# A two-layer graph transformer on one core: scores and values of two head pairs at a time

## What is computed

```
# layer 0: 8 heads of 64 features
Q, K, V = x @ W_q + b_q, x @ W_k + b_k, x @ W_v + b_v
scores = Q K^T / 8 + (a_i + c_j + b_g + log(adj + 1e-9))    # a, c = x @ w_g halves
x1 = softmax(scores) V + x
# layer 1: one head of 512 features, masked where adj == 0
scores = (x1 @ Wq + bq) (x1 @ Wk + bk)^T / sqrt(512)
ctx = softmax(masked scores) x1 @ Wc
out = layernorm(x1 + ctx) * gamma + beta
```

## Time and profile before

| | |
|---|---|
| median of three runs | 2368.58 us |
| time of the profiled execution itself | 2369.99 us |
| span of its profile, first to last instruction | 2368.2 us |
| PE busy | 2287.8 us (97%) |
| DVE busy | 1906.0 us (80%) |
| ACT, POOL busy | 1213.2 us (51%), 939.1 us (40%) |
| mean granted clock of PE | 0.989 of 2.4 GHz |
| DMA, mean share of its 16 engines | 35.9% |

### The profile page before, as it was taken

One profiled execution on the slowest core, in us unless ns is written; L12 is line 12 of the kernel. 1 busy time (PEld: TensorE's weight loads), 2 busy tenths in 40 slices (PEclk: granted clock), 3 DMA queues, 4 the chain that ended last, 5 costly groups with the idle time before them and its releaser, 6 DMA issues.

```text
span 2368.2 us, 39148 instructions
## 1 busy us (share of the span) xinstructions
PE 2287.8 (97%) x13268; PEld 1876.8 (79%) x13268; DVE 1906.0 (80%) x5507; ACT 1213.2 (51%) x3474; POOL 939.1 (40%) x1146
## 2 busy tenths in 40 slices
PE   7999999999999999999999999999999999999986
PEld 4788888888888888888888888888888888888874
DVE  4587888888888888888888888888888888887776
ACT  4545455545455545455545555544555554555542
POOL 0133345433345433445433444433444433344423
PEclk8999999999999999999999999999999999999997
DMA  6333343333343333343333334333334333333221
GB/s 223 107 94 118 123 125 120 121 107 111 121 134 121 115 113 109 124 134 121 107 121 107 125 123 131 100 123 113 125 124 130 99 120 117 124 122 127 88 81 45
DMA packets 187304, 277.97 MB, mean 117 GB/s; under 512 B 24672, under 2 KB 122592, under 8 KB 182880
## 3 DMA queue, kind: packets, MB, share of 16 engines
q1 hardware_dynamic: 187104, 275.47, 35.9%
HBM read 166.54 MB, written 108.86 MB: 116 GB/s over the span
## 4 chain that ended last, share of the span: by engine, by line
PE 72%; DVE 22%; POOL 3%; issue 1%; SPq 1%; DMA 0%; ACT 0%; DVEq 0%
PE bank L213 19%; PE bank L215 19%; PE bank L214 19%; PE bank L474 5%; PE bank L497 5%; PE bank L461 5%; DVE bias L942 4%; DVE x1n L1109 3%; DVE bnst L1112 3%; POOL probs L1247 3%; DVE xn L1004 2%; DVE probs L958 2%; DVE scratch L1001 2%; DVE turned L977 2%; DVE y_lo L1103 2%
## 5 line engine op out<-in xcount | busy, mean ns | idle before, releaser
L1247 POOL TENSOR_TENSOR probs<-probs,rcp 128x512 f32<-128x512 f32 x256 | 261.5, 1042 | 1184.5 <-DVE rcp L968 1184.5
L734 ACT ACTIVATE probs<-probs,nmax 128x128 f32<-128x128 f32 x1024 | 397.2, 391 | 264.0 <-DVE nmax L958 264.0
L1029 DVE STREAM_TRANSPOSE x1n<-x1T 32x512 f32<-32x512 f32 x512 | 359.8, 703 | 60.6 <-DMA out<-x1n 53.5
L755 ACT ACTIVATE g_sb<-bank,consts 128x512 f32<-128x512 f32 x128 | 88.1, 689 | 316.5 <-PE bank L215 314.7
L213 PE MATMUL bank<-wv_hi,x_hi 128*128 128x512 f32 x512 | 203.4, 397 | 34.1 <-DVE x1n L1109 32.6
L958 DVE CUSTOM_DVE_ANT_0 probs<-bank,bias 128x128 f32<-128x128 f32 x1024 | 227.2, 286 | 1.4
L1255 POOL TENSOR_TENSOR x_lo<-xT_land,x_hi 128x512 fp32r<-128x512 f32 x124 | 169.9, 1406 | 145.7 <-ACT x_hi L688 145.7
L213 PE MATMUL bank<-x_hi,wm_hi 128*128 128x512 f32 x512 | 205.6, 402 | 9.7 <-DVE x_lo L990 9.7
L977 DVE STREAM_TRANSPOSE turned<-probs 128x1024 f32<-128x1024 f32 x128 | 158.7, 1240 | 69.5 <-POOL probs L1247 68.5
L213 PE MATMUL bank<-x_hi,wk_hi 128*128 128x512 f32 x512 | 205.9, 402 | 7.3 <-DVE x_lo L901 7.3
L213 PE MATMUL bank<-wc_hi,x_hi 128*128 128x512 f32 x512 | 204.3, 399 | 0.0
(11 more groups left out here) (129 smaller groups left out, 5362.9 us busy)
## 6 DMA issues: line engine op xcount, KB each, us to landing
turn_dram<-turned SPq DMA_DIRECT2D x128, 512.0 KB, 2.6
probsT<-turn_dram SPq DMA_DIRECT2D x512, 128.0 KB, 2.7
out<-x1n SPq DMA_DIRECT2D x128, 256.0 KB, 2.2
xn<-in_x SPq DMA_DIRECT2D x126, 256.0 KB, 4.1
xT_land<-in_xT SPq DMA_DIRECT2D x31, 1024.0 KB, 5.2
adj_sb<-in_adj SPq DMA_DIRECT2D x32, 256.0 KB, 3.2
c_rows<-c_dram SPq DMA_DIRECT2D x32, 256.0 KB, 4.5
at_dram<-scratch SPq DMA_DIRECT2D x31, 256.0 KB, 2.0
```

Of the source, the lines that this page charges most:

```text
L734: op = nc.scalar.activation(probs[:, k, :], probs[:, k, :], ACT.Exp, bias=nmax[:, k:k + 1], scale=-1.0, accum_out=sums[:, k:k + 1])
L1029: op = nc.vector.transpose(x1n[b * BLK:(b + 1) * BLK, :, :] .rearrange("p g (c a s) -> p a c g s", c=C, a=P // BLK)[:, a, :, :, :], x1T[a ...
L1247: nc.gpsimd.tensor_tensor(probs[:, half, :], probs[:, half, :], rcp[:, half].unsqueeze(2).to_broadcast([P, HALF, P]), ALU.mult)\
```

## The change

PE does the scores and the values of two head pairs in one visit: `pv(u, 2)`, `pv(u, 3)`, `scores(t, 0)`, `scores(t, 1)` in the first, and `pv(t, 0)`, `pv(t, 1)`, `scores(t, 2)`, `scores(t, 3)` in the second. For this `q_sb` and `k_sb` exist twice, the scores of even pairs go to banks 4 and 5 and those of odd pairs to 6 and 7, and all other banks are dealt out anew. The programs of all engines stand in a new order. The first step merges its visits too, and has the four `m_chunk` (fp32 matmuls that make the merged matrix m) in one row. ACT takes the logarithm of a step's adjacency in that step, not at the end of the step before (`this_log_adj`), and `a_c` is kept twice for it. `x1_rows` comes in four parts instead of two, `row_term` one graph at a time. POOL does all four `affine` in a row and `next_x_low` ahead of `probabilities(t, 2)`. SP stores the four output rows in a row and issues `move_probs(t, 2)` behind `move_attention` and `spread_c`. No instruction that computes is added or left out.

The core of the diff:

```diff
-        q_sb = sb("q_sb", [P, COLS])
-        k_sb = sb("k_sb", [P, COLS])
+        q_sb = [sb(f"q_sb{i}", [P, COLS]) for i in range(2)]
+        k_sb = [sb(f"k_sb{i}", [P, COLS]) for i in range(2)]
         v_sb = sb("v_sb", [P, GG, D])
...

+        def k_bank(c):
+            return bank[(0, 2, 2, 0)[c]]
+
+        def q_bank(c):
+            return bank[(1, 3, 3, 1)[c]]
+
+        def s_banks(c):
+            return (bank[4], bank[5]) if c % 2 == 0 else (bank[6], bank[7])
+
+        def pv_bank(c, last=False):
+            return bank[(4 if last else 2) + c % 2]
+
         def g_bank(c, last):
-            return bank[(2, 3, 0, 1)[c] if last else 2 + c % 2]
+            return bank[(0, 1, 2, 3)[c] if last else (2, 3, 0, 1)[c]]

         def sa_bank(last):
-            return bank[6 if last else 7]
+            return bank[4]

         def y_bank(g, last):
-            return bank[((4, 5, 2, 3) if last else (2, 3, 1, 0))[g]]
+            return bank[(6, 7, 0, 1)[g] if last else g]

         def y_split(g, last):
...
             def scores(t, c):

                 pe.wait_ge(s["act_q"], nth("act_q", t, c))
                 pe.wait_ge(s["act_k"], nth("act_k", t, c))
-                if c > 0:
-                    pe.wait_ge(s["dve_max"], nth("dve_max", t, 2 * c - 1))
+                if c >= 2:
+                    pe.wait_ge(s["dve_max"], nth("dve_max", t, 2 * (c - 2) + 1))
                 elif t > 0:
...
                 project_k(0, 1)
                 project_q(0, 1)
+                pe.wait_ge(s_lo["v"], C)
+                pe.wait_ge(s["act_k"], nth("act_k", 0, 0))
+                project_v(0, 0)
+                pe.wait_ge(s["act_q"], nth("act_q", 0, 0))
+                project_v(0, 1)
+                scores(0, 0)
                 scores(0, 1)
-                m_chunk(1)
                 project_v(0, 2)
                 project_v(0, 3)
-                m_chunk(2)
-                project_k(0, 2)
-                project_q(0, 2)
-                pe.wait_ge(s_lo["m"], 3)
+                for d in range(C):
+                    m_chunk(d)
+                for c in range(2, 4):
+                    pe.wait_ge(s_lo["m"], 2 * c - 3)
+                    project_k(0, c)
+                    pe.wait_ge(s_lo["m"], 2 * c - 2)
+                    project_q(0, c)
+                pe.wait_ge(s["act_k"], nth("act_k", 0, 2))
                 pv(0, 0)
+                pe.wait_ge(s["act_q"], nth("act_q", 0, 2))
+                pv(0, 1)
                 scores(0, 2)
-                m_chunk(3)
+                scores(0, 3)
                 m_row_term()
-                project_k(0, 3)
-                project_q(0, 3)
                 m_columns()
-                pe.wait_ge(s["dve_pv"], nth("dve_pv", 0, 0))
-                pv(0, 1)
-                scores(0, 3)
...
+                    if c == 0:
+                        pe.wait_ge(s["dve_x1"], nth("dve_x1", u, 3))
+                    elif c >= 2:
+                        pe.wait_ge(s["act_v"], nth("act_v", t, c))
...
+                project_q(t, 1)
+                pe.wait_ge(s["act_k"], nth("act_k", t, 0))
                 project_v(t, 0)
-                scores(t, 0)
+                pe.wait_ge(s["act_q"], nth("act_q", t, 0))
+                project_v(t, 1)
+                pe.wait_ge(s["act_k"], nth("act_k", t, 1))
+                pv(u, 2)
+                pe.wait_ge(s["act_q"], nth("act_q", t, 1))
+                pv(u, 3)
                 if w >= 0:
                     pe.wait_ge(s["dve_res"], nth("dve_res", w, 3))
-                project_v(t, 1)
-                project_k(t, 1)
-                project_q(t, 1)
-                if w >= 0:
-                    pe.wait_ge(s["dve_res"], nth("dve_res", w, 2))
-                else:
-                    pe.wait_ge(s["dve_pv"], nth("dve_pv", u, 1))
-                pv(u, 2)
-                if w >= 0:
-                    pe.wait_ge(s["dve_sa"], nth("dve_sa", w))
-                else:
-                    pe.wait_ge(s_lo["m"], 4)
-                pv(u, 3)
+                scores(t, 0)
                 scores(t, 1)
-                project_k(t, 2)
                 project_v(t, 2)
                 project_v(t, 3)
                 gw(0)
                 gw(1)
...
+                project_k(t, 2)
                 project_q(t, 2)
-                pe.wait_ge(s["dve_pv"], nth("dve_pv", u, 2))
+                pe.wait_ge(s["act_g"], nth("act_g", u, 2))
+                project_k(t, 3)
+                pe.wait_ge(s["act_g"], nth("act_g", u, 3))
+                project_q(t, 3)
+                pe.wait_ge(s["act_k"], nth("act_k", t, 2))
                 pv(t, 0)
+                pe.wait_ge(s["act_q"], nth("act_q", t, 2))
+                pv(t, 1)
+                pe.wait_ge(s["dve_sa"], nth("dve_sa", u))
                 scores(t, 2)
+                scores(t, 3)
                 yw(0)
                 yw(1)
-                project_k(t, 3)
-                project_q(t, 3)
-                pe.wait_ge(s["dve_pv"], nth("dve_pv", t, 0))
-                pv(t, 1)
-                scores(t, 3)
+                yw(2)
                 pe.wait_ge(s["dve_tp"], nth("dve_tp", u))
+                pe.wait_ge(s["dve_max"], nth("dve_max", t, 5))
                 context(u, 0)
                 context(u, 1)
-                yw(2)
                 yw(3)
...

-            def next_log_adj(it):
-                act.wait_ge(s["dve_b"], nth("dve_b", it.t))
-                log_adj(it.t + 1, it.p + 1 + it.par, 1 - it.par)
+            def this_log_adj(it):
+                act.wait_ge(s["dve_b"], nth("dve_b", it.t - 1))
+                log_adj(it.t, it.p + 1, it.par)

             def layer1_alone(u):
...
                 q_out(t, 0)
-                exps(t, 0, 0)
+                k_out(t, 1)
                 if w >= 0:
                     norm(w, 2)
                     norm(w, 3)
-                exps(t, 0, 1)
-                k_out(t, 1)
                 q_out(t, 1)
+                this_log_adj(it)
                 act.wait_ge(s["pe_pv"], nth("pe_pv", u, C - 1))
                 v_out(t, 0)
                 v_out(t, 1)
                 x1hi(u, 2)
                 x1hi(u, 3)
+                exps(t, 0, 0)
+                v_out(t, 2)
+                exps(t, 0, 1)
+                v_out(t, 3)
+                g_out(u, 0, False)
                 exps(t, 1, 0)
+                g_out(u, 1, False)
+                exps(t, 1, 1)
+                g_out(u, 2, False)
+                g_out(u, 3, False)
+                exp1(u)
                 k_out(t, 2)
...
-                turn(u, 3)
                 if w >= 0:
                     residual1(w, 2)
-                bias(t)
+                turn(u, 3)
                 if w >= 0:
                     residual1(w, 3)
                 x1lo(u, 0)
                 x1lo(u, 1)
-                maxima(t, 0)
                 if it.nxt:
                     next_gate(t + 1, 0)
                     next_gate(t + 1, 1)
-                recips(t, 0)
+                bias(t)
                 residual0(u, 2)
                 residual0(u, 3)
-                turn(t, 0)
-                maxima(t, 1)
+                maxima(t, 0)
                 x1lo(u, 2)
                 x1lo(u, 3)
                 x1_rows(u, 0)
+                recips(t, 0)
+                x1_rows(u, 1)
+                turn(t, 0)
+                maxima(t, 1)
+                x1_rows(u, 2)
+                x1_rows(u, 3)
                 recips(t, 1)
-                x1_rows(u, 1)
+                row_term(u, 0)
+                row_term(u, 1)
                 turn(t, 1)
-                row_terms(u, False)
+                row_term(u, 2)
+                row_term(u, 3)
                 masked_scores(u, False)
-                residual0(t, 0)
+                if it.nxt:
+                    next_gate(t + 1, 2)
                 attention1(u)
                 turn_attention(u)
+                residual0(t, 0)
+                residual0(t, 1)
                 maxima(t, 2)
-                y_low(u, 0, False)
-                recips(t, 2)
-                y_low(u, 1, False)
-                if it.nxt:
-                    next_gate(t + 1, 2)
-                turn(t, 2)
-                att1T_low(u, False)
-                maxima(t, 3)
-                residual0(t, 1)
                 if it.nxt:
                     next_gate(t + 1, 3)
+                recips(t, 2)
+                y_low(u, 0, False)
+                att1T_low(u, False)
+                y_low(u, 1, False)
+                turn(t, 2)
+                maxima(t, 3)
+                residual1(u, 0)
                 y_low(u, 2, False)
-                residual1(u, 0)
                 y_low(u, 3, False)
                 residual1(u, 1)
...
-                    affine(w, 1)
+                    for g in range(1, GG):
+                        affine(w, g)
                 if it.l0:
                     probabilities(t, 0)
-                if w >= 0:
-                    affine(w, 2)
```

(5 more changed lines are left out.)

278 lines of the change are left out of this document (127 added, 151 removed).

## The result

The changed kernel takes 2340.77 us (median of four runs, 2337.67 to 2343.91); the kernel before takes 2368.33 beside it. The ratio is 0.9885, 95% interval 0.9868 to 0.9902: 27 us faster, 1.15%, where 79 were forecast, and outside the range that ended at 2325. The profiled execution is the one of 2337.67 us, with a span of 2335.9. The forecast's sign was right; the gain is a third of its size.

What follows compares the result with a forecast made beforehand. PE was taken as the bound. Savings of 1.05 (step 1), 64.2 (steps 2 to 31), 12.3 (first step) and 2.1 (last) sum to 79.7 us: span 2288.5, time 2289 us, range 2277 to 2325.

Steps and rivals of the forecast that it cites:

- What bounds the kernel: Steady steps: PE is the bound, a step is its queue's sum, going from 71.30 to 69.16 us.
- the chain to gw(0): Steady step: logarithm, bias, residuals, maxima and x1lo end at 24.5 to 25.6, 1.6 to 2.7 us before gw(0).
- The list of chains: Four chains checked against PE's new order: pv(u, 3), gw(0), context(u, 0) and context 3, with 1.3 to five us spare.
- context 3 with 1.3: Next step's context 3 at 72.5 needs residual1(u, 1), ready at 71.2: 1.3 us to spare, the tightest chain.
- three places where a new wait would show it wrong: PE waiting ahead of gw(0) for L994, context 0 for the low attention, or context 3 for L1113, count 30.
- Some of the slack is not there: Rival, 20%: DVE still waits 7.9 us from pv(u, 3) to first context; up to 1.4 us late per step, 2331 us.
- Visits: PE's visits for scores and values, four become two: 1.05 us less per step, 33 us over 31 steps.
- The wait: PE's wait for residual1 on bank 3 goes: 1.09 us less per step, if nothing is late instead.
- The first step: k(1, 0) starts at 78.1 instead of 90.36, 12.3 us saved, with 2.9 added for a slower clock.
- Its rival for this step: Rival, 5%: the first step keeps its length because its DVE chain is the bound; 2289 + 10 = 2299 us.
- The last step: residual1(w, 2) ahead of turn(u, 3) fills DVE's wait for POOL's probabilities: 2.1 us saved.

Runs made afterwards that it cites:

- Four versions: Changed kernel with sigmas ahead of the affine; with early logarithm and swapped g_out; with all three; sigmas version without most affine: 2290.33, 2293.31, 2289.78, 2287.83 us.
- all three edits: Changed kernel with sigma(w, 2), sigma(w, 3) ahead of affine(w, 0), this_log_adj behind x1hi(u, 1), and g_out(u, 1) ahead of exps(t, 1, 0): 2289.78 us, ratio 0.9668.
- the sigmas first: Changed kernel with sigma(w, 2) and sigma(w, 3) moved ahead of affine(w, 0) on POOL: 2290.33 us, ratio 0.9666.
- The swap of the two calls: Changed kernel with g_out(u, 1) ahead of exps(t, 1, 0) on ScalarE, the logarithm left where it is: 2324.29 us, ratio 0.9813.
- the early logarithm: Changed kernel with this_log_adj moved on ScalarE from behind q_out(t, 1) to behind x1hi(u, 1), ahead of norm(w, 0): 2293.81 us, ratio 0.9686.
- two moved calls in the kernel before: Kernel before the change with project_v(t, 1) and its wait moved behind project_q(t, 1), still four visits: 2334.41 us, ratio 0.9858.

## Why the prediction was wrong

**What bounds the kernel** was right: PE's queue, and 69.16 us per step is what it adds up to. Four versions reach 69.13. With all three edits the kernel takes 2289.8 us, where the prediction gave 2289. It was the price of the change under the condition that nothing is late, and that condition failed.

**The step that failed** is the chain to gw(0): "ACT can take the logarithm behind q1, at 13.7 to 14.8 ... it ends near 16.6", and from it "So I cost the new orders, the doubled buffers and SP's new sequence at nothing". The logarithm's length was right (2.0 with its table load). What stands ahead of it was left out of the sum: between k1 and q1 on ACT stand norm(w, 2) and norm(w, 3), and they wait 2.96 and 0.83 us for POOL, whose sigmas stand behind an affine of 2.9 us. I checked when PE had made q1, and not when ACT came to it. That is 1.8 us. The second part is the bias, taken as 3.13 from the earlier trace rows; the longer wait put it entirely beside POOL's affines, where it lasts 4.42: 1.3 us. Together they used up what gw(0) had (1.6 to 2.7 in the forecast; it is just late) and what `g_out(u, 1)` had. The runs show that the first part decides: with the sigmas first the bias lasts 4.70 and PE waits for nothing. What the longer bias alone would have cost isn't shown, since no run shortens it in the changed kernel with the logarithm late.

**The list of chains** lacked the one that broke first. `g_out(u, 1)` behind `exps(t, 1, 0)` isn't among the four. By the forecast's own times it would have had 1.6 us to spare: maxima(t, 1) at 33.3, its first half 0.85 earlier, four `exps` of 0.39 and a copy of 0.67 make 34.7, and PE asks at 36.3. So listing it would not alone have saved the number, but it would have shown a second chain, as short as the first, on the same logarithm. The tightest in the list, context 3 with 1.3, never waited in a steady step. The swap of the two calls shows what the place is worth: 0.5 of 1.6 us per step, and most of the rest comes out at `k_out(t, 2)`. The prediction named three places where a new wait would show it wrong, and this one is not among them either.

**The rival** "Some of the slack is not there" is what happened, by the amount that it had worked out as its upper end: 1.4 us late per step, 2331 us. A typical step is 1.41 late; with the steps that lose a further half microsecond the mean is 1.6, and the time 2340.8. That the two 1.4 agree is luck. The rival's reason was a different one: it had DVE fuller and kept the 7.9 us of waiting as a block. The experiments show it is not DVE's load: with the early logarithm DVE has the same instructions in the same order, and what falls is its wait and the length of the bias (busy for 1667 us of the 29 steps instead of 1739); with the sigmas first its bias is even longer. It was given 20% and only half of its reach in the range.

**Visits**: right, 1.01 for 1.05. The term was formed per visit, "four visits (0.48 + 3 x 0.57) become two"; the runs show that it sits per change of shape, eleven before and six after, 1.01 / 5 = 0.20 each, 0.17 between the two small shapes. The two ways agree here and part elsewhere: another full block between pv and scores costs 0.21, not 0.57. The Trainium skill ("TensorE: Matmul & The Clock Gate", Step-by-step) gives about 128 cycles as the drain behind the last column of any matmul, not as the price of a change of mode; taken as that price, as the prediction's estimate did, five changes were 0.27 us, and the measured 1.01 is nearly four times that.

**The wait** for `residual1`: right, 1.16 for 1.09. From start to start it is 1.16 before the change too (1.36 us from the last matmul of the scores to the next one, where it is 0.20 without the wait); the bracket in the earlier trace rows says 1.09, and the 0.07 between them had gone to the visit of scores alone.

**The first step**: 13.1 us saved for 12.3. The slower clock cost 1.8 us there and not 2.9, and DVE's `v_b`, as forecast, sets the start of k(1, 0). The prediction had its rows of the clock mixed up: the stretch from 28 to 36 us at 0.61 comes behind a wait of 4.5 us for a DMA, and the wait of 3.25 for q comes later, with 0.50 from 44.7 to 48 us behind it; so the clock is low behind each, and the conclusion stands. Its rival for this step adds 10 us where its own sum had 12.3. **The last step**: 0.5 us for 2.1, since `x1lo` there moved beside POOL's affine.

What stays open: why the attention's trip through DRAM is a microsecond longer in some steps, and whether that also makes the wider spread of the changed kernel's runs (0.27% against 0.1% before). The runs on time have it too and lose nothing by it, up to 2.0 us of waiting.

## What to carry to other kernels

When an operation is moved to a new place in an engine's queue, its start is the end of whatever now stands ahead of it on that queue, and those waits must be followed into every other engine, the least busy one too: here an affine of 2.9 us ahead of the sigmas on POOL decided about 50 us on PE, and one moved call gave them back. Spare time that several chains share through one operation (here the logarithm) is one risk and not several, so if one of them is late, the range has to hold the whole loss, in every step. And try the smallest part alone: two moved calls in the kernel before gave at least as much as the whole change as it stood.
